# Second feed-forward of a linear-attention stack in three float32r passes over high and low parts

## The reference, cut to what matters

```
for i in range(8):
    residual = x
    Q  = elu(x @ Wq[i] + bq[i]) + 1          # 16 heads of 64
    Kf = elu(x @ Wk[i] + bk[i]) + 1
    V  = x @ Wv[i] + bv[i]
    KV, sumK = sum(Kf * V, tokens), sum(Kf, tokens)
    att = Q * KV / (Q * sumK + 1e-6)
    x = layer_norm(gelu(att @ Wo[i] + bo[i]) + residual)     # y1, z1, n1, x1
    h = gelu(x @ W1[i] + b1[i])                              # 128 -> 512, hid
    h = gelu(h @ W2[i] + b2[i])                              # 512 -> 128, y2
    x = layer_norm(h + x)                                    # z2, n2, the new state
```

## Time and profile before

| | |
|---|---|
| runs of the kernel | 3437.15, 3437.23, 3439.71 us; median 3437.23 |
| the profiled execution's own time | 3444.96 us |
| its span | 3443.2 us, 51737 instructions |
| PE busy | 3047.9 us, 89% |
| DVE busy | 2762.6 us, 80% |
| ACT busy | 2417.9 us, 70% |
| POOL busy | 575.6 us, 17% |
| TensorE's mean granted clock | 0.94 of full speed |

### The profile page before, as it was taken

The page is one execution under the profiler, slowest core; times in us unless marked ns, Lnnn a source line. Parts: engine busy times, 40 slices in busy tenths (PEclk is TensorE's granted clock), DMA queues, the critical chain, the costliest instruction groups (busy, mean ns, idle before and its releaser), DMA issues. The chain is left out here.

```text
span 3443.2 us, 51737 instructions
## 1 busy us (share of the span) xinstructions
PE 3047.9 (89%) x14384; PEld 1990.4 (58%) x14384; DVE 2762.6 (80%) x10898; ACT 2417.9 (70%) x4441; POOL 575.6 (17%) x695
## 2 busy tenths in 40 slices
PE   6999998272699999999999999999999999999668
PEld 5777776161466565565655656666565665666342
DVE  5878777843589898898888889898898988998454
ACT  5888876031488878887877878878788878888420
POOL 0000001383111121121111111111111211211110
PEclk9999998585899999999999999999999999999769
DMA  1000000322100000000000000000000000000000
GB/s 53 1 1 1 1 0 13 100 35 36 61 1 1 25 8 1 19 10 5 1 25 8 1 19 13 2 1 25 8 1 25 13 2 1 1 1 1 0 4 22
DMA packets 31650, 46.94 MB, mean 14 GB/s; under 512 B 5320, under 2 KB 21760, under 8 KB 31360
## 3 DMA queue, kind: packets, MB, share of 16 engines
q1 hardware_dynamic: 25728, 39.46, 3.4%
q0 software_dynamic: 5632, 4.20, 0.9%
HBM read 35.16 MB, written 8.49 MB: 13 GB/s over the span
## 5 line engine op out<-in xcount | busy, mean ns | idle before, releaser
L1776 DVE TENSOR_SCALAR t_feat_q<-t_recip,t_neg_mean 128x256 f32<-128x256 f32 x1024 | 392.1, 444 | 137.4 <-ACT t_recip L1632 130.2
L1479 PE MATMUL t_o_ps<-t_feat_q,t_wo 128*128 128x512 f32 x1024 | 482.9, 605 | 14.2 <-issue 11.6
L1624 ACT ACTIVATE t_recip<-t_feat_q,t_z_scale 128x256 f32<-128x256 f32 x1024 | 434.7, 498 | 1.8 <-DVE t_feat_q L1776 1.0
L1610 ACT ACTIVATE t_exp_k<-t_k_ps 128x1024 f32<-128x1024 f32 x256 | 260.0, 1016 | 250.3 <-PE t_k_ps L1456 250.3
L1739 DVE CUSTOM_DVE_ANT_0 t_junk<-t_v_ps,t_feat_k 128x256 f32<-128x256 f32 x1024 | 390.3, 418 | 20.7 <-PE t_v_ps L1456 20.5
L1729 DVE SCALAR_TENSOR_TENSOR t_feat_k<-t_exp_k,t_k_ps 128x256 f32<-128x256 f32 x1024 | 368.9, 416 | 29.9 <-ACT t_exp_k L1610 29.8
L1614 ACT ACTIVATE t_exp_q<-t_q_ps 128x1024 f32<-128x1024 f32 x256 | 261.7, 1022 | 95.0 <-PE t_q_ps L1456 94.7
L1765 DVE SCALAR_TENSOR_TENSOR t_feat_q<-t_exp_q,t_q_ps 128x1024 f32<-128x1024 f32 x256 | 312.6, 1221 | 8.9
L1479 PEld LDWEIGHTS t_o_ps<-t_feat_q,t_wo 128*128 128x128 f32 x1024 | 196.3, 193 | 192.9 <-issue 172.4
L1454 PE MATMUL t_v_ps<-t_x_hi,t_w_hi 128*128 128x512 f32 x512 | 266.7, 521 | 26.8 <-DVE t_w_lo L1720 17.0
L1902 POOL TENSOR_TENSOR t_var_eps<-t_moments,t_ln_eps 128x4 f32<-128x4 f32 x128 | 70.1, 548 | 1266.4 <-DVE t_moments L1787 1266.4
(11 more groups left out here) (353 smaller groups left out, 7138.1 us busy)
## 6 DMA issues: line engine op xcount, KB each, us to landing
t_raw_w<-in_wk SPq DMA_DIRECT2D x8, 512.0 KB, 3.6
t_raw_w<-in_wq SPq DMA_DIRECT2D x8, 512.0 KB, 4.4
t_raw_w<-in_wv SPq DMA_DIRECT2D x8, 512.0 KB, 5.4
t_raw_o<-in_wo SPq DMA_DIRECT2D x8, 512.0 KB, 4.0
t_raw<-in_w SPq DMA_DIRECT2D x16, 256.0 KB, 2.7
x<-in_x SPq DMA_DIRECT2D x4, 512.0 KB, 6.8
tokens_dram<-r_hn SPq DMA_DIRECT2D x8, 256.0 KB, 2.3
e_w_raw<-in_fc_w SPq DMA_DIRECT2D x4, 512.0 KB, 4.1
```

The source lines that it names most:

```text
L1479: last = pe.matmul(o_ps[:], wo[:, chunk, :], feat_q[:, s, chunk, :], start=(chunk == 0), stop=(chunk == NC - 1), skip_group_check=True)
L1610: act.activation(exp_k[:], k_ps[:], ACT.Exp, bias=-1.0).then_inc(c["k_exp"], 1)
L1624: last = act.activation(recip[:, q % 2, k * UNIT + n * SEQ:k * UNIT + (n + 1) * SEQ], feat_q[:, s, chunk, cols], ACT.Ln, bias=1.0, scale=z ...
L1776: last = dve.tensor_scalar(feat_q[:, s, chunk, cols], recip[:, q % 2, k * UNIT + n * SEQ:k * UNIT + (n + 1) * SEQ], -1.0, neg_mean[:, s, n ...
```

## The change

The hidden values and the second weights are each split into a high part, rounded to float32r, and a low part, the rest. The second feed-forward becomes, for each quarter j, three float32r passes: high by high, low weights by high values, high weights by low values. ScalarE rounds (`round_hidden`, an `ACT.Copy` per quarter, the first in front of gelu 1, the second between gelus 2 and 3, the last two behind gelu 3), Pool subtracts (`split_hidden`, four subtractions, in its program ahead of `rstd_of` for E). Pool's `swap_w2` makes two parts instead of one copy. The waits follow: a gelu waits until the split of its quarter in the unit before has read `hid`, a rounding until the second feed-forward of the unit before is done, TensorE for each quarter's split.

```diff
-        w2 = sb("t_w2", [P, NF, D])
+        w2_hi = sb("t_w2_hi", [P, NF, D], F32R)
+        w2_lo = sb("t_w2_lo", [P, NF, D], F32R)
...
+        hid_hi = sb("t_hid_hi", [P, NF, UNIT], F32R)
+        hid_lo = sb("t_hid_lo", [P, NF, UNIT], F32R)
...
                 for j in range(NF):
-                    last = pe.matmul(m0[:], w2[:, j, :], hid[:, j, :], start=(j == 0), stop=(j == NF - 1))
+                    pe.wait_ge(c["hid_split"], 4 * u + j + 2)
+                    pe.matmul(m0[:], w2_hi[:, j, :], hid_hi[:, j, :], start=(j == 0), stop=False)
+                    pe.matmul(m0[:], w2_lo[:, j, :], hid_hi[:, j, :], start=False, stop=False)
+                    last = pe.matmul(m0[:], w2_hi[:, j, :], hid_lo[:, j, :], start=False, stop=(j == NF - 1))
                 last.then_inc(c["w2_filled"], 1)
...
             def first_gelu(u, j):
 
                 act.wait_ge(c["w1_filled"], 4 * u + j + 2)
+                if not isinstance(u, int) or u >= 1:
+                    act.wait_ge(c["hid_split"], 4 * u + j - 2)
                 act.activation(hid[:, j, :], (m1, m0)[j % 2][:], ACT.Gelu_apprx_tanh, bias=param(u, 1 + j)).then_inc(c["hid_ready"], 1)
+
+            def round_hidden(u, j):
+
+                if not isinstance(u, int) or u >= 1:
+                    act.wait_ge(c["w2_filled"], u + 1)
+                act.wait_ge(c["hid_ready"], 4 * u + j + 2)
+                act.activation(hid_hi[:, j, :], hid[:, j, :], ACT.Copy).then_inc(c["hid_hi_ready"], 1)
...
                 if Dn:
+                    round_hidden(t - 3, 0)
                     first_gelu(t - 3, 1)
...
                 if Dn:
                     first_gelu(t - 3, 2)
+                    round_hidden(t - 3, 1)
                     first_gelu(t - 3, 3)
+                    round_hidden(t - 3, 2)
+                    round_hidden(t - 3, 3)
...
             def swap_w2(layer):
                 pool.wait_ge(c["raw_2_in"], 16 * layer + 17)
                 carry(2)
-                copy(w2[:], raw_2[:]).then_inc(c["w2_ready"], 1)
+                copy(w2_hi[:], raw_2[:]).then_inc(c["w2_hi_ready"], 1)
+                pool.wait_ge(c["w2_hi_ready"], layer + 2)
+                pool.tensor_tensor(w2_lo[:], raw_2[:], w2_hi[:].bitcast(F32), ALU.subtract).then_inc(c["w2_ready"], 1)
+
+            def split_hidden(u):
+                if not isinstance(u, int) or u >= 1:
+                    pool.wait_ge(c["w2_filled"], u + 1)
+                for j in range(NF):
+                    pool.wait_ge(c["hid_hi_ready"], 4 * u + j + 2)
+                    pool.tensor_tensor(hid_lo[:, j, :], hid[:, j, :], hid_hi[:, j, :].bitcast(F32), ALU.subtract).then_inc(c["hid_split"], 1)
...
+                if Dn:
+                    split_hidden(t - 3)
                 if E:
                     rstd_of(t - 4, 1, c["stats2_ready"], c["var2_ready"], c["rstd2_ready"])
```

## The result

| | before | after |
|---|---|---|
| median of the runs | 3438.47 us (4 runs, 3437.15 to 3440.57) | 3552.11 us (4 runs, 3549.52 to 3560.54) |
| ratio, with its 95% interval | | 1.0342 (1.0320 to 1.0364) |
| span of the profiled execution | 3443.2 us | 3547.8 us |
| busy PE, DVE, ACT, POOL | 89, 80, 70, 17% | 85, 82, 72, 26% |
| mean granted clock | 0.940 | 0.941 |

A forecast was written before the change was run, and what follows sets the result against it. The bound was taken to be a loop handed from engine to engine, 35.18 us a step. Per-step losses summed to 103.4 us, added to 3444.96 for 3548.4, less 7.7 gave 3541; range 3500 to 3605, about 0.83.

The forecast's parts named there:

- TensorE's 0.75, of which only VectorE's room counts: Second feed-forward: twelve passes take 0.75 us less per unit, but only VectorE's 0.19 us wait before keys 3 is gained.
- ScalarE: Four Copies among the first feed-forward's gelus: gelu 1 0.32 us late, gelu 3 and the turn of z2 0.84 late.
- table load: Rival: Copies among gelus cost three table loads of 1.28 us, about 234 us in all, 3775; chance 0.04.
- Pool: Splits 1 to 3 stand ahead of the variance of z2, which begins 1.88 us late, containing ScalarE's 0.84.
- VectorE's wait for the root: Sign before VectorE's normalise: its wait for Pool grows from 0.49 to some 1.5 us.
- z1's addition: VectorE's addition falls among splits 1 to 3 and is held, but its turn ends before the normalise; costed at nothing.
- The port rival: z1's addition slips in ahead of split 3, Pool's chain up to 0.66 us longer in 53 steps: +35, 3576; chance 0.14.
- The swap step: Pool's swap of w2 gets one more subtraction, about 1.4 us, costed at nothing; step counted as ordinary, +1.69 us.
- At the end of the loop body: Seven steps where TensorE waits 1.83 us for its own issue: its 0.75 counts in full, +1.13 us each.
- Where a layer opens: Seven steps: 1.37 us plus 0.6 for split 0 near VectorE's subtraction of the low weights, together +1.97 each.
- The sum: 46 ordinary steps at 1.69, 7 at 1.97, 7 at 1.13, four short ones at 1 each: 103.4 us.
- The clock: Rival: TensorE's new idle time near the turns lowers its clock; one step in four hit gives 3570; chance 0.12.

The follow-up runs named there:

- e1: Kernel before with the twelve float32r passes alone, no Copies or splits of hidden values, low hidden part left out: step 34.87 us, median 3424.17 us, ratio 0.9956.
- e2: Kernel after, but the second feed-forward multiplies in plain float32 as before; Copies, splits and waits stay: step 37.07 us, median 3558.01 us, ratio 1.0346.
- e3: Kernel after with Pool's splits 1 to 3 moved behind the variance and root of z2: step 36.14 us, median 3512.16 us, ratio 1.0213.
- e5: e3 with split 3 also waiting for VectorE's subtraction of one from the queries' exponential: step 35.63 us, median 3469.74 us, ratio 1.0095.
- e6: e5 plus e4's order on ScalarE, and one ScalarE exponential moved behind the state write: step 35.08 us, median 3444.50 us, ratio 1.0024.
- e4: Kernel after with all four ScalarE roundings behind gelu 3, Pool's order unchanged: steps 38.5 and 40.2 us, median 3691.66 us, ratio 1.0735.
- e8: Kernel before with only Pool's x_lo subtraction made to wait for VectorE's attention on quarter 1: step 35.18 us, median 3426.25 us, ratio 0.9960.

## Why the prediction was right

The forecast was 3541 and its sum for the span 103.4; the span grew by 104.6. The median came 11 us higher than forecast, since the profiled execution after is the lowest of its runs and that of before lay 7.7 above the median. Step by step:

- *TensorE's 0.75, of which only VectorE's room counts.* Right, though it was 0.63: in e1 and e2 the passes are worth 0.31 of it. The room was read as 0.19 and is 0.31: 0.27 on VectorE, as a wait also costs the overlap of the instructions around it, and 0.04 that is open.
- *ScalarE.* Right: gelu 2 was 0.26 later (0.32 predicted), gelu 3 0.78 (0.84), without a table load. That rival is gone.
- *Pool.* Right: the variance began 1.82 later (1.88), right behind three subtractions of 1.25 each, and this lateness contains ScalarE's. e3 and e5 show both parts: 1.13 goes with Pool's order, 0.76 stays as ScalarE's. One sign to look for was wrong: VectorE's wait for the root stays at 0.49 and does not grow to 1.5, since the held addition of z1 and the sums over values behind it fill the time.
- *z1's addition.* It was held, 1.79 us, and its turn ended (1834.87) before the normalise of 1835.34. It costs nothing there. The port rival, by which Pool would be held, did not come there: split 3 starts at 1832.31 and the addition at 1832.37, behind it. The Trainium skill, "SBUF — State Buffer", Who interferes with whom, says that whichever starts first keeps the shared pair for its whole instruction and the other blocks; 1.79 against 0.66 agrees. Only 0.05 to 0.07 us between the two starts, in every full step, kept the rival out, and that was luck. The other order does occur once in the kernel after, in the first step in which a layer opens: VectorE's subtraction starts 0.02 us ahead of split 0 and takes its usual time, and split 0 takes 2.33 us instead of 1.29.

```profile
1168.33 1.23 DVE L1739 TENSOR_TENSOR t_w_lo<-t_raw_w,t_w_hi 128x1024 fp32r<-128x1024 f32 x1
```

```profile
1168.35 2.33 POOL L1926 TENSOR_TENSOR t_hid_lo<-t_hid,t_hid_hi 128x512 fp32r<-128x512 f32 x1 [9.69 <-ACT t_hid_hi L1616]
```

- *The other steps were under-sized.* The swap step lost 1.88 to 1.90 and not 1.69: VectorE is late there anyway, so the passes give nothing, as e1 shows. At the end of the loop body TensorE's gain was to count in full (+1.13); five of the seven steps lost 1.5 to 1.95. TensorE's wait for issue is 2.20 (1923.40) where it was 1.83, so 0.37 of the 0.63 is waited for there, and 1.88 - 0.26 = 1.62. The seventh has no such wait and lost 1.55. Where a layer opens, in six of the seven, split 0 does not hold the low weights' subtraction itself but a tiny instruction in front of it, with the same effect:

```profile
1781.91 1.00 DVE L1778 SCALAR_TENSOR_TENSOR t_neg_mean<-t_kv_all,t_inv_sum 128x16 f32<-128x16 f32 x1
1782.84 1.21 DVE L1739 TENSOR_TENSOR t_w_lo<-t_raw_w,t_w_hi 128x1024 fp32r<-128x1024 f32 x1
```

```profile
1784.18 0.79 PE L1457 MATMUL t_v_ps<-t_x_hi,t_w_hi 128*128 128x512 f32 x1 [3.24 <-DVE t_w_lo L1739]
```

  TensorE waits 0.82 longer than in the earlier trace rows, where 0.6 was put.
- *The sum* held because the misses cancel, which is luck: opening steps 5.6 and loop ends 3.9 too cheap; the ordinary and swap steps 77.7 (46 of them) against 72.7 (45), and the ends 4 against 0.6, too dear.
- *The clock* is the same over the whole span (0.940 and 0.941), but not step by step, and the sum has no term for that. Windows of two steps at the end of the loop body, from state write to state write, before and after (columns as in rows 1):

```profile
2750.49:2787.26 36.77, 34.66 (x142) 21.68 (x141) 31.04 (x125) 29.20 (x41) 5.70 (x6) 1.00 0.01 3
1576.33:1614.97 38.64, 36.35 (x142) 22.22 (x141) 31.03 (x125) 29.20 (x42) 5.71 (x6) 0.96 0.01 3
```

```profile
2834.14:2874.66 40.52, 36.00 (x146) 22.95 (x145) 33.19 (x125) 31.13 (x46) 10.83 (x10) 0.96 0.01 3
1607.20:1645.69 38.49, 34.31 (x146) 22.35 (x145) 33.18 (x125) 31.11 (x45) 10.84 (x10) 1.00 0.01 3
```

  The first of each pair is the step that lost 3.74: there the clock fell in the kernel after alone. The second lost nothing (-0.15): there it fell in the kernel before alone. Three of the seven opening steps lost 2.8 to 3.8 instead of 2.3, and only in these three is the granted clock lower than before (0.92 against 0.96 in two, 0.89 against 0.92 in the third). By an estimate from these steps that is some 4 us of the 104.6. What decides whether the clock falls in such a step is open.

## What to carry to other kernels

Where a loop is handed from engine to engine, a saving counts only as far as the next engine in the loop has room, and added work costs in full where it stands in an in-order queue ahead of an instruction on the loop; the same four subtractions cost 1.13 us a step ahead of the variance and nothing where e5 puts them. When moving work on Pool, look at what VectorE does at that time as well as at Pool's own queue: a place that is free on Pool held VectorE for 1.1 us. Moving the work out of both ways, instead of dropping the change, turned 3.4% slower into 0.9% faster, 0.4 of which belongs to `x_lo` alone.

## What was not expected of the hardware

- Pool's subtraction of 128x512 held small instructions of VectorE like large ones, where they started behind it: 128x16 took 1.28 us instead of 0.17 (1822.57 against e6's 1823.42), and one with a single tile as input took 1.77 instead of 0.66 (e3). Pool itself took 1.29 to 1.31 in these rows; where VectorE had started first, Pool's took 2.33.
- A wait just under 3 us in front of a small turn brought TensorE down to 1.2 GHz in both steps of e4 that are shown, once within the turn and once behind it; a wait of 1.83 us for issue at the end of the loop body did so in the kernel before, and one of 1.83 at the same place in e8 (2748.22) did not. In e1 a wait of 2.42 (1296.83) did, with 0.61 granted in the 4 us behind it, and one of 2.43 (2459.73) did not, with 1.00; one of 3.15 in e6 (2180.18) did not either: the four matmuls behind it took 1.98 us. The length of the wait alone does not tell.
